# Attention row maxima taken with queries on partitions, the softmax shift carried in two halves, six places for transposed tokens

## The chip, the cores and the metric

The kernel runs on one core of a Trainium2 chip. The metric is device time in microseconds (us) of one execution. The kernel before the change took 273.44 us in the median of 3 runs (272.13 to 273.6).

## The reference

For each of 16 batches of 256 tokens of width 128 the reference does one post-norm transformer layer in float32:

```python
qkv = x @ attn_w.T + attn_b                     # 16 heads of 8; 256 tokens per batch
scores = einsum('bhki,bhqi->bhkq', k, q) / sqrt(8)
scores = where(key <= query, scores, -10000.0)
probs = softmax(scores, axis=key)
x = layernorm(x + (einsum('bhkq,bhkl->bhql', probs, v) heads joined) @ out_w.T + out_b)
# feed-forward: int8 quantised rows of x times int8 quantised columns of rhs
x = layernorm(x + (round(x / sx) @ round(rhs / sr)) * sx * sr)
```

`sx` is the largest absolute value of a token's row over 127, `sr` that of a column of `rhs`.

## The kernel before, in words

Each engine runs its own program, in order, and they meet only at semaphores. All programs walk the same list of phases, b = -4 to 18, and inside a phase the compute engines walk ten units u = 0 to 9. A unit is one PSUM bank of 128 x 512 scores: two halves of 64 partitions (heads 4*half + p%4) and 512 columns. The causal upper triangle of 256 x 256 scores is cut into 64-wide key blocks; FULL, ENDS and THIRD name which key blocks of which head pairs a unit holds. Units 0 to 4 are head pairs 0 to 3 (row tile 0 of the PE array), units 5 to 9 are pairs 4 to 7 (row tile 64).

Scores are computed twice. The first time, for the **maxima**, the bank goes to VectorE (DVE), which takes maxima (`maxima`, L643). The second time, for the **exponentials**, two more rows of the contraction (`DEPTH = ROWS + 2`) subtract a **shift** per group of 32 queries, written as bfloat16 plus remainder, and ScalarE (ACT) exponentiates the bank (L470). `max_unit` sets the lead of the maxima: beside the exponentials of (b, u) PE makes the scores for the maxima of unit u+5, so units 5 to 9 of batch b+1 and then units 0 to 4 of batch b+2. The two kinds use opposite row tiles and run side by side (`scores`).

Before the change both kinds keep keys on partitions, and the maxima go over 32 queries with a transposing reduce. `join_maxima` (after u = 4) reduces over the three kinds of unit, PE turns the result (`turn_maxima`, at u = 5), and `make_shift` (DVE, u = 5) reduces again and makes the two bfloat16 parts. Two DMAs write them into the query rows (`load_shift`, L340), and PE waits for them before the exponentials of the next batch's unit 0 (`bank_for_exp`).

**PSUM rings.** ACT has 4 banks and DVE 3, handed out in the fixed order of `ring_places`: the ten units, and after certain units an extra place (`ACT_EXTRAS`, `DVE_EXTRAS`). PE may fill a place only when the place three back (DVE) or four back (ACT) was emptied. DVE's order has four extras per phase: the output projection after u = 1, the feed-forward after 3, the shift after 5, the turned PV result after 6.

**Who does what in a phase b.** PE, after the scores of the unit named: u = 1 output projection of batch b-2, PV products of b-1, turn of the quantised tokens of b-3; u = 3 query and key projection of b+4 (L933, reads `xt_in`), PV, feed-forward of b-3; u = 5 `turn_maxima(b+1)` and value projection of b+1 (L943, also reads `xt_in`); u = 6 turn of the PV result, PV; u = 8 turn of the heads, PV. DVE has at the matching units the first sum and its statistics (1, 2), the scaling of the feed-forward (3), join (4), shift (5), division by the denominators and the token scale (6), statistics and the second bfloat16 part of q and k (7, 8). GpSimd (POOL) splits q and k into bfloat16 parts and makes the norm factors.

**SP's queue** issues every DMA of the loop, in this order, each waiting for its data in turn:

```python
write_image(b + 3, 1); load_x(b); load_shift(b + 1); read_image(b + 3)
load_xt(b + 5); write_image(b + 4, 0); store(b - 3)
```

`write_image` and `read_image` send the parts of q and k through DRAM into the layout that the scores need. `load_xt(b + 5)` refills one of 4 places of `xt_in` (transposed tokens) and waits until ACT has read the value projection of batch b+1; the query and key projection of b+5 comes in phase b+1 at u = 3. The first four token blocks are loaded ahead of the loop.

Of the kernel before, what the change touches and what calls it, by code (L numbers as in the profile page):

```python
# [59 lines left out]
QK_RING, XT_RING, RING = 4, 4, 3  # L60
# [25 lines left out]

PV_GROUPS = [(0, 1), (2, 3, 4), (5, 6), (7, 8, 9)]
# [7 lines left out]
ACT_EXTRAS = {1: [("zq", -3)], 3: [("q", 4), ("k", 4)], 5: [("v", 1)], 8: [("heads", -1)]}  # L95
DVE_EXTRAS = {1: [("out", -2)], 3: [("ffn", -3)], 5: [("shift", 1)], 6: [("pv", -1)]}
# [38 lines left out]
def build_program(nc, x, xt, wqkv_t, bqkv, wo_t, bo, rhs_t, out):  # L135
    ctx = ExitStack()
    with ctx:
# [26 lines left out]
        causal = sb("causal", [128, KB], BF16)  # L164
        minus_half = sb("minus_half", [128, TILES])
# [62 lines left out]
        shift_loaded = sem("shift_loaded")  # L228
# [44 lines left out]
        POOL_MASK = 9  # L273
# [5 lines left out]
        def _(sp):  # L279
# [6 lines left out]
            for b in range(2, XT_RING):  # L286
                sp.dma_start(xt_in[b][:, :], xt[b]).then_inc(xt_loaded[b], 16)

            def load_xt(b):
                if not real(b) or b < XT_RING:  # L290
# [42 lines left out]
            def load_shift(b):  # L333
                if not real(b):
                    return
                wait_place(sp, dve_emptied, DVE_AT, ("shift", b))
# [26 lines left out]
        def _(pool):  # L363
# [10 lines left out]
            step(pool.memset(causal[:, :], MASKED))  # L374
            step(pool.memset(ones[:, :], 1.0))
# [4 lines left out]
            for half in range(2):  # L380
                m = causal[64 * half:64 * half + 64, :]
                step(pool.affine_select(out=m, in_=m, compare_op=ALU.is_gt, fill=0.0,
                                        base=0, pattern=[[-1, KB]], channel_multiplier=1))
# [79 lines left out]
        def _(act):  # L463
# [112 lines left out]
            def phase(b):  # L576
                for u in range(NU):
                    exponentials(b, u)
                    if u == 1:
                        pv_from_psum(b - 1)  # L580
                        zq_from_psum(b - 3)
                    if u == 3 and b > -4:
                        qk_from_psum(b + 4, 0)
                        qk_from_psum(b + 4, 1)
                    if u == 5:
                        v_from_psum(b + 1)
                        norm1(b - 2)
                    if u == 8:
                        heads_from_psum(b - 1)
                    if u == 9:  # L590
                        round_z(b - 2)
# [5 lines left out]
        def _(dve):  # L597
# [6 lines left out]
            dve.memset(part_max[:, :, :, :], MASKED).then_inc(rows_set, 1)  # L604
# [27 lines left out]
            def maxima(b, u):  # L632
# [5 lines left out]
                first, last = ((0, 8), (2, 10), (4, 8))[kind]  # L638
                out32 = part_max[:, kind, p0:p0 + (4 if kind == THIRD else 2), first:last]
                if u == 0:  # L640
                    wait(dve, max_joined, b - 1)
# [4 lines left out]
            def join_maxima(b):  # L646
                if not real(b):
                    return
                wait_place(dve, dve_emptied, DVE_AT, ("max", b, NU - 1))
                wait_place(dve, dve_filled, DVE_AT, ("shift", b - 1))  # L650
                by_pair = key_max[:, :].rearrange("k (p c) -> k p c", c=8)
                dve.tensor_reduce(by_pair, part_max[:, :, :, 0:8].rearrange("k n p c -> k p c n"),  # L652
                                  op=ALU.max, axis=AX.X).then_inc(max_joined[1], 1)
                wait(dve, max_joined, b, 1)
                dve.tensor_tensor(by_pair[:, :, 6:8], by_pair[:, :, 6:8], part_max[:, 1, :, 8:10],  # L655
                                  ALU.max).then_inc(max_joined[1], 1)
# [6 lines left out]
            def make_shift(b, step):  # L663
# [3 lines left out]
                at = DVE_AT["shift", b]  # L667
                turned = dve_bank[at % DVE_BANKS]
                if step == 0:
                    dve.wait_ge(dve_filled, at + 1)  # L670
                    dve.tensor_reduce(turned[:, 64:96], turned[:, 0:64].rearrange("c (w q) -> c q w", w=2),
                                      op=ALU.max, axis=AX.X, negate=True).then_inc(shift_made[1], 1)
                elif step == 1:
                    wait(dve, shift_made, b, 1)
                    if b > 0:
                        dve.wait_ge(shift_loaded, 32 * b)
                    dve.tensor_copy(shift[:, 0, :], turned[:, 64:96]).then_inc(shift_made[1], 1)
                else:
                    wait(dve, shift_made, b, 2)
                    dve.tensor_tensor(shift[:, 1, :], turned[:, 64:96], shift[:, 0, :],  # L680
                                      ALU.subtract).then_inc(dve_emptied, 1)
# [85 lines left out]
            def phase(b):  # L767
                if b == -3:
                    second_part(1)
                for u in range(NU):  # L770
                    maxima(*max_unit(b, u))
                    if u == 1:
# [4 lines left out]
                    if u == 3:  # L777
                        scale_ffn(b - 3)
                    if u == 4:
                        join_maxima(b + 1)  # L780
                    if u == 5:
                        make_shift(b + 1, 0)
                        make_shift(b + 1, 1)
                        make_shift(b + 1, 2)
# [7 lines left out]
                    if u == 8:  # L792
                        second_stats(b - 3, 1)
# [31 lines left out]
        def _(pe):  # L825
# [14 lines left out]
            def piece_scores(b, u, i, half, bank, depth):  # L840
# [3 lines left out]
                rows, slot = slice(row, row + depth), b % QK_RING  # L844
                pe.matmul(bank[64 * half:64 * half + 64, at:at + TOK - blk * KB],  # L845
                          k_stat[slot][rows, head, blk * KB:(blk + 1) * KB], q_move[slot][rows, head, blk * KB:TOK],
                          start=(at == 0), stop=False, skip_group_check=True)

            def own_blocks(u, half, bank):


                kind, p0 = UNITS[u]
                row, each = TILE_ROWS * (p0 // 4), 1 if kind == FULL else 2
                rows, keys = slice(row, row + KB), slice(64 * half, 64 * half + 64)
                columns = bank[keys, :].rearrange("k (p n q) -> k p n q", p=2, q=KB)[:, :, 0:(1, 4, 4)[kind]:(1, 3, 2)[kind], :]
                return pe.matmul(columns, identb[rows, rows],  # L856
                                 causal[rows, :].unsqueeze(1).unsqueeze(1).to_broadcast([KB, 2, each, KB]),
# [9 lines left out]
            def bank_for_exp(b, u):  # L867
                if u == 0:
                    pe.wait_ge(shift_loaded, 32 * (b + 1))
                return act_ring(("exp", b, u))  # L870

            def scores(b, u):
# [6 lines left out]
                for i in range(len(pieces(u))):  # L879
                    for half in range(2):  # L880
                        if for_max:
                            piece_scores(of_max, unit, i, half, max_bank, ROWS)
                        if for_exp:
                            piece_scores(b, u, i, half, exp_bank, DEPTH)
                for half in range(2):
                    if for_max:
                        own = own_blocks(unit, half, max_bank)
                        if half == 1:
                            own.then_inc(dve_filled, 1)
                    if for_exp:  # L890
                        own = own_blocks(u, half, exp_bank)
# [23 lines left out]
            def turn_maxima(b):  # L915
                if not real(b):
                    return
                wait(pe, max_joined, b)
                bank = dve_ring(("shift", b))
                for s in range(2):  # L920
                    for half in range(2):
                        rows = slice(64 * s + 32 * half, 64 * s + 32 * half + 32)
                        last = pe.matmul(bank[rows, 0:64], key_max[:, 32 * s:32 * s + 32], ident[:, 64 * half:64 * half + 64],  # L923
                                         start=True, stop=True)
                last.then_inc(dve_filled, 1)
# [89 lines left out]
            def phase(b):  # L1015
# [3 lines left out]
                for u in range(NU):  # L1019
# [5 lines left out]
                    if u == 3:  # L1025
                        if b >= -1:
# [47 lines left out]
```

## Time and profile before

| | |
|---|---|
| median of 3 runs | 273.44 us |
| profiled execution, its own time | 273.3 us |
| its span (first to last instruction) | 271.6 us |
| PE busy | 203.1 us, 75% |
| DVE busy | 186.8 us, 69% |
| ACT busy | 161.1 us, 59% |
| POOL busy | 135.2 us, 50% |
| mean granted TensorE clock | 0.952 |

Busy shares are means over a start (to about 42 us), a steady part, and a drain (from about 234 us), and tell little alone. To read a stage, cut the trace at an event that comes once per phase. Here it is the start of DVE's L652, the join after u = 4: it comes at 27.6 us in phase -1 and at 234.3 us in phase 14.

### The profile page before, as it was taken

The page shows a single profiled execution, that of the slowest core. Times are in us where ns is not written, and L with a number is a line of the kernel's source. Part 1 is how long each engine was busy: PE and PEld are TensorE (multiplying, and loading weights), DVE is VectorE, ACT ScalarE, POOL GpSimd, SP SyncE. Part 2 cuts the span into 40 slices and gives each one's busy share as a digit, 9 for nine tenths or more (in the row PEclk, how much of TensorE's full clock was granted, in tenths as well). Part 3 has the DMA queues.
Part 4 walks back from the last instruction along what each step waited for, and adds up shares of the span by engine and source line. Part 5 has one row for each costly group of instructions (what it writes and reads, how often), then busy time and mean ns, then how long its engine had stood idle before and what let it go on. Part 6 is the DMA issues. An engine that isn't in the chain of part 4 may idle for free.

```text
span 271.6 us, 10973 instructions
## 1 busy us (share of the span) xinstructions
PE 203.1 (75%) x4398; PEld 133.9 (49%) x4399; DVE 186.8 (69%) x545; ACT 161.1 (59%) x349; POOL 135.2 (50%) x268
## 2 busy tenths in 40 slices
PE   7269758689886868686878787777778879799610
PEld 4156635456564545454646455545455556565300
DVE  3727834746786869696969696868789899644521
ACT  3811133644685858585767665666767668678420
POOL 7352303231617473737474746474746262445764
PEclk9999999957999999999999999999999999899955
DMA  4499391909283848647675849391929550110001
GB/s 135 160 188 226 68 216 28 230 25 183 94 148 132 139 158 124 175 105 192 104 193 102 196 80 220 66 231 35 242 52 212 108 93 6 42 36 10 19 21 39
DMA packets 50754, 32.82 MB, mean 121 GB/s; under 512 B 7184, under 2 KB 50704, under 8 KB 50704
## 3 DMA queue, kind: packets, MB, share of 16 engines
q1 hardware_dynamic: 50560, 31.93, 52.1%
q8 instruction: 35, 0.57, 0.9%
q10 hardware_dynamic: 144, 0.20, 0.3%
q14 instruction: 15, 0.12, 0.2%
HBM read 17.17 MB, written 14.68 MB: 117 GB/s over the span
## 4 chain that ended last, share of the span: by engine, by line
PE 29%; DMA 25%; DVE 20%; ACT 8%; SPq 7%; issue 7%; POOL 3%; POOLq 0%; ACTq 0%; DVEq 0%
DMA xt_in<-xt_dram 22%; DVE part_max L643 9%; PE act_bank L933 7%; PE pv_bank L910 7%; PE dve_bank L845 4%; ACT z L518 3%; PE act_bank L943 3%; SPq L330 2%; DVE key_max L652 2%; DVE ffn L749 2%; SPq L331 2%; ACT probs L470 2%; DMA k_stat<-imagek 2%; SPq L340 2%; DVE key_max L655 2%
## 5 line engine op out<-in xcount | busy, mean ns | idle before, releaser
L643 DVE TRANSPOSE_TENSOR_REDUCE part_max<-dve_bank 128x16 f32<-128x512 f32 x160 | 108.7, 702 | 31.3 <-PE dve_bank L856 29.4
L470 ACT ACTIVATE probs<-act_bank 128x512 f32<-128x512 f32 x160 | 88.3, 595 | 31.1 <-PE act_bank L856 30.3
L845 PE MATMUL dve_bank<-q_move,k_stat 48*64 48x256 bf16 (+3 forms) x1024 | 67.1, 251 | 2.0 <-DMA k_stat<-imagek 1.8
L845 PE MATMUL act_bank<-q_move,k_stat 50*64 50x256 bf16 (+3 forms) x1024 | 63.6, 242 | 0.0
L845 PEld LDWEIGHTS dve_bank<-q_move,k_stat 48*64 48x64 bf16 x1024 | 42.5, 115 | 22.5 <-issue 10.2
L910 PE MATMUL pv_bank<-probs,v_stat 128*32 128x256 f32 (+3 forms) x1024 | 50.6, 318 | 0.3 <-ACT probs L470 0.2
L856 PE MATMUL dve_bank<-causal,identb 64*64 64x256 bf16 (+1 forms) x320 | 44.4, 270 | 0.6 <-issue 0.6
L856 PE MATMUL act_bank<-causal,identb 64*64 64x256 bf16 (+1 forms) x320 | 42.3, 260 | 0.0
L422 POOL TENSOR_SCALAR rstd<-moments 128x2 f32<-128x2 f32 x32 | 7.4, 230 | 69.3 <-DVE moments L765 53.8
L845 PEld LDWEIGHTS act_bank<-q_move,k_stat 50*64 50x64 bf16 x1024 | 39.9, 111 | 1.6 <-issue 0.6
L933 PE MATMUL act_bank<-xt_in,wqkv 128*128 128x256 f32 x64 | 22.6, 490 | 14.7 <-DMA xt_in<-xt_dram 14.3
L404 POOL TENSOR_TENSOR qk_parts<-qk_rest,qk_parts 128x512 bf16<-128x512 f32 x15 | 17.4, 1157 | 27.8 <-DVE qk_parts L661 27.8
L910 PEld LDWEIGHTS pv_bank<-probs,v_stat 128*32 128x32 f32 x1024 | 22.8, 113 | 15.9 <-issue 5.1
L482 ACT ACTIVATE qk_f<-act_bank,bias 128x256 f32<-128x256 f32 x30 | 13.1, 474 | 25.7 <-PE act_bank L933 25.6
L494 ACT ACTIVATE v_stat<-act_bank 64x256 f32<-64x256 f32 x32 | 12.1, 378 | 25.7 <-PE act_bank L943 25.5
L749 DVE SCALAR_TENSOR_TENSOR ffn<-dve_bank,zscale,rhs_scale 128x128 f32<-128x128 f32 x32 | 9.6, 342 | 20.9 <-PE dve_bank L994 20.9
L424 POOL TENSOR_TENSOR rstd<-rstd,minus_half 128x2 f32<-128x2 f32 x32 | 22.4, 700 | 2.7
L933 PEld LDWEIGHTS act_bank<-xt_in,wqkv 128*128 128x128 f32 x64 | 13.5, 231 | 20.0 <-DMA xt_in<-xt_dram 15.8
L856 PEld LDWEIGHTS dve_bank<-causal,identb 64*64 64x64 bf16 x320 | 20.2, 118 | 0.2
L923 PE MATMUL dve_bank<-ident,key_max 128*32 128x64 f32 x128 | 5.5, 246 | 19.8 <-DVE key_max L655 19.8
L856 PEld LDWEIGHTS act_bank<-causal,identb 64*64 64x64 bf16 x320 | 18.8, 112 | 0.9 <-issue 0.8
L399 POOL TENSOR_TENSOR qk_rest<-qk_f,qk_parts 128x512 f32<-128x512 f32 x15 | 17.4, 1157 | 1.2
(87 smaller groups left out, 312.4 us busy)
## 6 DMA issues: line engine op xcount, KB each, us to landing
imageq<-qk_parts SPq DMA_DIRECT2D x32, 192.0 KB, 3.6
imagek<-qk_parts SPq DMA_DIRECT2D x32, 192.0 KB, 4.0
q_move<-imageq SPq DMA_DIRECT2D x32, 192.0 KB, 3.9
k_stat<-imagek SPq DMA_DIRECT2D x32, 192.0 KB, 4.5
xt_in<-xt_dram SPq DMA_DIRECT2D x16, 128.0 KB, 4.8
x_in<-x_dram SPq DMA_DIRECT2D x16, 128.0 KB, 3.5
out_dram<-o SPq DMA_DIRECT2D x16, 128.0 KB, 3.1
q_move<-shift SPq DMA_DIRECT2D x32, 8.0 KB
```

The lines of the kernel that those rows point to most:

```text
L399: pool.tensor_tensor(qk_rest[:, :, :], qk_f[:, :, :], first, ALU.subtract).then_inc(qk_split[1], 1)
L404: pool.tensor_tensor(third, qk_rest[:, :, :], second, ALU.subtract).then_inc(qk_split[1], 1)
L424: pool.tensor_tensor(t[:, 0, :], t[:, 0, :], minus_half[:, :], ALU.pow).then_inc(made[1], 1)
L470: act.activation(probs[u][:, :], act_bank[at % ACT_BANKS][:, :], ACT.Exp, scale=SCALE).then_inc(act_emptied, 1)
L482: act.activation(qk_f[:, w, :], src, ACT.Identity, bias=bias[:, w:w + 1]).then_inc(act_emptied, 1)
L494: last = act.activation(v_stat[b % RING][half, :, :, 16 * s:16 * s + HD], src, ACT.Copy)
L643: dve.tensor_reduce(out32, dve_bank[at % DVE_BANKS][:, :].rearrange("k (c q) -> k c q", q=32), op=ALU.max, axis=AX.X, apply_transpose=True ...
L749: last = dve.scalar_tensor_tensor(out=ffn[:, t, :], in0=dve_bank[at % DVE_BANKS][:, t * DIM:(t + 1) * DIM], scalar=zscale[:, 1, t:t + 1], ...
L845: pe.matmul(bank[64 * half:64 * half + 64, at:at + TOK - blk * KB], k_stat[slot][rows, head, blk * KB:(blk + 1) * KB], q_move[slot][rows, ...
L856: return pe.matmul(columns, identb[rows, rows], causal[rows, :].unsqueeze(1).unsqueeze(1).to_broadcast([KB, 2, each, KB]), start=False, st ...
L910: last = pe.matmul(pv_bank[col:col + 32, p // 4, blk * KB:TOK], v_stat[b % RING][:, blk, p, :], probs[u][:, at:at + TOK - blk * KB], start ...
L933: pe.matmul(bank[:, 0:TOK], wqkv[:, w, :], xt_in[b % XT_RING][:, :], start=True, stop=True).then_inc(act_filled, 1)
```

## The change

The scores for the maxima are transposed: queries become the stationary operand and keys the moving one, so queries stand on partitions and an ordinary reduce along the free dimension ends each maximum (per block of 64 queries now). Which key blocks make a unit is mirrored, with the same number of columns per unit, and the mask has a transposed twin. The maxima are joined, turned and made into a shift for each half of the heads (row tile) separately, each half with its own place in DVE's ring (five extras per phase) and its own semaphore. `xt_in` has six places. Projections and DMAs move: value projection from u = 5 to u = 8, `load_xt` one phase earlier, and in phase -1 the query and key projection from u = 3 to u = 8.

```diff
-QK_RING, XT_RING, RING = 4, 4, 3
+QK_RING, XT_RING, RING = 4, 6, 3
+XT_FIRST = 4
+def max_pieces(u):
+    kind, p0 = UNITS[u]
+    if kind == FULL:
+        return [(p0 + j, 3, TOK * j) for j in range(2)]
+    if kind == ENDS:
+        return [(p0 + j, blk, TOK * j + at) for j in range(2) for blk, at in ((2, KB), (0, 0))]
+    return [(p0 + j, 1, 2 * KB * j) for j in range(4)]
-ACT_EXTRAS = {1: [("zq", -3)], 3: [("q", 4), ("k", 4)], 5: [("v", 1)], 8: [("heads", -1)]}
-DVE_EXTRAS = {1: [("out", -2)], 3: [("ffn", -3)], 5: [("shift", 1)], 6: [("pv", -1)]}
+ACT_EXTRAS = {1: [("zq", -3)], 3: [("q", 4), ("k", 4)], 8: [("heads", -1), ("v", 1)]}
+DVE_EXTRAS = {1: [("out", -2)], 3: [("shift0", 1), ("ffn", -3)], 6: [("pv", -1)], 8: [("shift1", 1)]}
-        part_max = sb("part_max", [128, 3, PAIRS, 10])
-        key_max = sb("key_max", [128, 64])
-        shift = sb("shift", [128, 2, 32], BF16)
+        ends_max = sb("ends_max", [128, PAIRS, 6])
+        query_max = sb("query_max", [128, PAIRS, 4])
+        shift = [sb(f"shift{s}", [16, 2, 128], BF16) for s in range(2)]
...
# SP
+            def load_shift(b, s):
...
                 for part in range(2):
-                    row = ROWS + part
-                    sp.dma_start(q_move[b % QK_RING][row:row + TILE_ROWS + 1:TILE_ROWS, :, :].rearrange("s f (c q) -> s (f c) q", q=32),
-                                 shift[:, part, :]).then_inc(shift_loaded, 16)
+                    row = s * TILE_ROWS + ROWS + part
+                    for half in range(2):
+                        heads_of_half = q_move[b % QK_RING][row:row + 1, 4 * half:4 * half + 4, :]
+                        sp.dma_start(heads_of_half.rearrange("r j t -> r (j t)"), shift[s][:, part, 64 * half:64 * half + 64]).then_inc(shift_loaded[s], 16)
             def phase(b):
                 write_image(b + 3, 1)
+                load_shift(b + 1, 0)
                 load_x(b)
-                load_shift(b + 1)
+                if b < 0:
+                    load_shift(b + 1, 1)
                 read_image(b + 3)
-                load_xt(b + 5)
+                load_xt(b + 6)
                 write_image(b + 4, 0)
+                if b >= 0:
+                    load_shift(b + 1, 1)
                 store(b - 3)
# DVE: maxima, join, shift
-                dve.tensor_reduce(out32, dve_bank[at % DVE_BANKS][:, :].rearrange("k (c q) -> k c q", q=32),
-                                  op=ALU.max, axis=AX.X, apply_transpose=True).then_inc(dve_emptied, 1)
+                dve.tensor_reduce(top, keys, op=ALU.max, axis=AX.X).then_inc(dve_emptied, 1)
+            def join_maxima(b, s):
...
+                wait_place(dve, dve_emptied, DVE_AT, ("max", b, 5 * s + 4))
+                dve.tensor_reduce(query_max[:, pairs, 0:4:2], ends_max[:, pairs, :].rearrange("q p (n k) -> q p n k", n=2),
+                                  op=ALU.max, axis=AX.X).then_inc(max_joined[1], 1)
+            def make_shift(b, s):
...
+                turned = dve_bank[at % DVE_BANKS][0:16, 0:128]
+                dve.wait_ge(dve_filled, at + 1)
+                if b > 0:
+                    dve.wait_ge(shift_loaded[s], 64 * b)
+                dve.tensor_scalar(shift[s][:, 0, :], turned, -1.0, None, ALU.mult).then_inc(shift_made[1], 1)
+                wait(dve, shift_made, b, s + 1)
+                dve.scalar_tensor_tensor(out=shift[s][:, 1, :], in0=turned, scalar=-1.0, in1=shift[s][:, 0, :],
+                                         op0=ALU.mult, op1=ALU.subtract).then_inc(dve_emptied, 1)
# DVE, phase: joins after u = 0 (half 0) and u = 5 (half 1) in place of u = 4;
#             shifts after u = 3 (half 0) and u = 8 (half 1) in place of u = 5
# ACT, phase: v_from_psum(b + 1) after u = 8 in place of u = 5
# PE
+            def max_scores(b, u, i, half, bank):
+                p, blk, at = max_pieces(u)[i]
+                row, head = TILE_ROWS * (p // 4), 4 * half + p % 4
+                rows, slot, keys = slice(row, row + ROWS), b % QK_RING, (blk + 1) * KB
+                pe.matmul(bank[64 * half:64 * half + 64, at:at + keys],
+                          q_move[slot][rows, head, blk * KB:keys], k_stat[slot][rows, head, 0:keys],
+                          start=(i == 0), stop=False, skip_group_check=True)
             def bank_for_exp(b, u):
-                if u == 0:
-                    pe.wait_ge(shift_loaded, 32 * (b + 1))
+                if u == 0 or u == 5:
+                    pe.wait_ge(shift_loaded[u // 5], 64 * (b + 1))
+            def turn_maxima(b, s):
...
+                bank = dve_ring((f"shift{s}", b))
+                pe.matmul(bank[0:16, 0:128], query_max[:, 4 * s:4 * s + 4, :].rearrange("q p n -> q (p n)"), ident[:, :],
+                          start=True, stop=True).then_inc(dve_filled, 1)
                     if u == 3:
-                        if b >= -1:
+                        turn_maxima(b + 1, 0)
+                        if b >= 0:
                             project_qk(b + 4, 0)
                             project_qk(b + 4, 1)
-                    if u == 5:
-                        turn_maxima(b + 1)
-                        project_v(b + 1)
                     if u == 8:
+                        turn_maxima(b + 1, 1)
+                        if b == -1:
+                            project_qk(b + 4, 0)
+                            project_qk(b + 4, 1)
                         turn_heads(b - 1)
+                        project_v(b + 1)
```

## Rows read from the trace of the kernel before

**Rows 1.** The page's chain that ended last, share of the span by line.

```profile
DMA xt_in<-xt_dram 22%; DVE part_max L643 9%; PE act_bank L933 7%; PE pv_bank L910 7%; PE dve_bank L845 4%; ACT z L518 3%; PE act_bank L943 3%; SPq L330 2%; DVE key_max L652 2%; DVE ffn L749 2%; SPq L331 2%; ACT probs L470 2%; DMA k_stat<-imagek 2%; SPq L340 2%; DVE key_max L655 2%
```

**Rows 2.** The chain from 138 to 168 us: start us, us, what.

```profile
152.57 1.13 PE act_bank L933 x4
...
157.88 0.52 SPq L340
...
161.32 5.68 DMA xt_in<-xt_dram
```

**Rows 3.** Windows cut at L652's starts: busy us (count) by engine, clock, DMA.

```profile
core 0: us, PE busy (x) PEld busy (x) DVE busy (x) ACT busy (x) POOL busy (x), PEclk, DMA share, GB/s
...
27.60:42.60 15.00, 11.09 (x168) 7.77 (x168) 8.10 (x16) 4.75 (x10) 4.49 (x6) 1.00 0.55 125
42.60:57.60 15.00, 11.71 (x260) 7.41 (x260) 7.97 (x16) 7.64 (x16) 4.17 (x6) 0.89 0.56 126
57.60:72.00 14.40, 12.84 (x270) 8.67 (x270) 9.92 (x25) 7.92 (x17) 3.57 (x8) 0.76 0.59 131
...
85.60:99.80 14.20, 10.96 (x274) 7.26 (x274) 11.19 (x34) 9.63 (x22) 8.41 (x17) 1.00 0.66 143
...
184.40:198.50 14.10, 10.96 (x274) 7.26 (x274) 11.17 (x34) 9.60 (x22) 8.39 (x17) 1.00 0.58 144
...
222.50:234.30 11.80, 10.08 (x268) 6.69 (x267) 10.60 (x33) 9.16 (x20) 4.85 (x13) 1.00 0.13 33
```

**Rows 4.** Waits, whole span: engine line waited for, total us, times, longest.

```profile
PE dve_bank L923 <- DVE key_max L655: 19.8, 16, 1.5
...
PE act_bank L933 <- DMA xt_in<-xt_dram: 14.3, 12, 2.7
```

**Rows 5.** DVE's timeline in one steady phase: start, us, [idle before it].

```profile
141.05 0.71 DVE L643 TRANSPOSE_TENSOR_REDUCE part_max<-dve_bank 128x16 f32<-128x512 f32 x1
...
145.32 0.42 DVE L732 TENSOR_REDUCE zscale<-z 128x2 f32<-128x256 f32 x1 [0.41 <-ACT z L518]
...
148.22 1.91 DVE L643 TRANSPOSE_TENSOR_REDUCE part_max<-dve_bank 128x16 f32<-128x512 f32 x3
...
151.43 0.72 DVE L643 TRANSPOSE_TENSOR_REDUCE part_max<-dve_bank 128x16 f32<-128x512 f32 x1 [0.47 <-PE dve_bank L856]
...
154.53 0.61 DVE L749 SCALAR_TENSOR_TENSOR ffn<-dve_bank,zscale,rhs_scale 128x128 f32<-128x128 f32 x2 [1.65 <-PE dve_bank L994]
155.06 0.70 DVE L643 TRANSPOSE_TENSOR_REDUCE part_max<-dve_bank 128x16 f32<-128x512 f32 x1
```

**Rows 6.** DVE by line and form: shapes, count, busy us, mean ns.

```profile
L643 DVE TRANSPOSE_TENSOR_REDUCE part_max<-dve_bank 128x16 f32<-128x512 f32 x160 | 108.7, 702 | 31.3 <-PE dve_bank L856 29.4
L749 DVE SCALAR_TENSOR_TENSOR ffn<-dve_bank,zscale,rhs_scale 128x128 f32<-128x128 f32 x32 | 9.6, 342 | 20.9 <-PE dve_bank L994 20.9
...
L732 DVE TENSOR_REDUCE zscale<-z 128x2 f32<-128x256 f32 x16 | 6.7, 418 | 8.5 <-ACT z L518 8.5
...
L652 DVE TENSOR_REDUCE key_max<-part_max 128x64 f32<-128x192 f32 x16 | 6.1, 381 | 0.5
...
L655 DVE TENSOR_TENSOR key_max<-key_max,part_max 128x16 f32<-128x16 f32 x16 | 4.4, 273 | 0.6
...
L671 DVE TENSOR_REDUCE dve_bank<-dve_bank 128x32 f32<-128x64 f32 x16 | 3.3, 203 | 0.4 <-PE dve_bank L923 0.4
```

**Rows 7.** PE's timeline in the same phase.

```profile
149.08 0.68 PE L975 MATMUL dve_bank<-wo,heads_d 128*128 128x128 f32 x4 [0.75 <-DVE part_max L643]
...
152.57 0.48 PE L933 MATMUL act_bank<-xt_in,wqkv 128*128 128x256 f32 x1 [0.84 <-DMA xt_in<-xt_dram]
```

**Rows 8.** Shift and token transfers: issue durations, landing, the first shift's landing.

```profile
L340 SPq DMA_DIRECT2D q_move<-shift x32: 512/517/660, 29.8 to 236.6; - x32
...
DMA to landing us min/median/max: 4.2/5.1/5.7
...
29.83 1.22 SPq L340 DMA_DIRECT2D q_move<-shift  x2
...
32.54 0.42 PE L845 MATMUL act_bank<-q_move,k_stat 50*64 50x256 bf16 x1
```

More of the change, by code:

```diff
@@ L227, in build_program @@
         qk_loaded = [sem(f"qk_loaded{i}") for i in range(QK_RING)]
-        shift_loaded = sem("shift_loaded")
+        shift_loaded = [sem(f"shift_loaded{s}") for s in range(2)]
         stored = sem("stored")
@@ L285, in _ @@
             sp.dma_start(rhst[:, :], rhs_t).then_inc(rhs_in, 16)
-            for b in range(2, XT_RING):
+            for b in range(2, XT_FIRST):
                 sp.dma_start(xt_in[b][:, :], xt[b]).then_inc(xt_loaded[b], 16)
             def load_xt(b):
-                if not real(b) or b < XT_RING:
+                if not real(b) or b < XT_FIRST:
                     return
@@ L380, in _ @@
             for half in range(2):
[L381 to L383 removed]
+                for m, sign in ((causal, 1), (causal_t, -1)):
+                    m = m[64 * half:64 * half + 64, :]
+                    step(pool.affine_select(out=m, in_=m, compare_op=ALU.is_gt, fill=0.0,
+                                            base=0, pattern=[[-sign, KB]], channel_multiplier=sign))
             assert done[0] == POOL_MASK, done[0]
@@ L646, in join_maxima @@
-            def join_maxima(b):
+                if kind == FULL:
+                    top = query_max[:, p0:p0 + 2, 3]
+                elif kind == ENDS:
+                    top = ends_max[:, p0:p0 + 2, 2:6]
+                else:
+                    top = query_max[:, p0:p0 + 4, 1]
+                if u == 0 or u == 5:
+                    wait_place(dve, dve_filled, DVE_AT, (f"shift{u // 5}", b - 1))
+                dve.wait_ge(dve_filled, at + 1)
+                keys = dve_bank[at % DVE_BANKS][:, :]
@@ L771, in phase @@
                     maxima(*max_unit(b, u))
+                    if u == 0:
+                        join_maxima(b + 1, 0)
                     if u == 1:
@@ L838, in dve_ring, with exp_scores, own_blocks @@
                 return dve_bank[at % DVE_BANKS]
-            def piece_scores(b, u, i, half, bank, depth):
+            def exp_scores(b, u, i, half, bank):
                 p, blk, at = pieces(u)[i]
                 row, head = TILE_ROWS * (p // 4), 4 * half + p % 4
-                rows, slot = slice(row, row + depth), b % QK_RING
+                rows, slot = slice(row, row + DEPTH), b % QK_RING
                 pe.matmul(bank[64 * half:64 * half + 64, at:at + TOK - blk * KB],
                           k_stat[slot][rows, head, blk * KB:(blk + 1) * KB], q_move[slot][rows, head, blk * KB:TOK],
[L847 to L855, printed above, removed]
+                          start=(i == 0), stop=False, skip_group_check=True)
[5 more added lines that the diff above has]
+                          q_move[slot][rows, head, blk * KB:keys], k_stat[slot][rows, head, 0:keys],
+                          start=(i == 0), stop=False, skip_group_check=True)
+            def own_blocks(u, half, bank, own, mask):
+                row = TILE_ROWS * (UNITS[u][1] // 4)
+                rows, out = slice(row, row + KB), slice(64 * half, 64 * half + 64)
+                columns = bank[out, :].rearrange("k (p n q) -> k p n q", p=2, q=KB)[:, :, own, :]
                 return pe.matmul(columns, identb[rows, rows],
-                                 causal[rows, :].unsqueeze(1).unsqueeze(1).to_broadcast([KB, 2, each, KB]),
+                                 mask[rows, :].unsqueeze(1).unsqueeze(1).to_broadcast([KB, 2, 1 if UNITS[u][0] == FULL else 2, KB]),
                                  start=False, stop=True, skip_group_check=True)
@@ L890, in scores @@
                     if for_exp:
-                        own = own_blocks(u, half, exp_bank)
+                        own = own_blocks(u, half, exp_bank, EXP_OWN[UNITS[u][0]], causal)
                         if half == 1:
@@ L913, in pv @@
                 last.then_inc(pv_done[1], 1)
-            def turn_maxima(b):
+            def turn_maxima(b, s):
                 if not real(b):
                     return
[L918 to L925, printed above, removed]
+                wait(pe, max_joined, b, s + 1)
+                bank = dve_ring((f"shift{s}", b))
+                pe.matmul(bank[0:16, 0:128], query_max[:, 4 * s:4 * s + 4, :].rearrange("q p n -> q (p n)"), ident[:, :],
+                          start=True, stop=True).then_inc(dve_filled, 1)
             def project_qk(b, w):
```

60 lines of the change are left out of this document (20 added, 40 removed).

## The prediction, as put on record before the changed kernel was run

> **What bounds the kernel now.** I read the chain of waits first. Its largest line is the load of the transposed tokens, 22% of the span [rows 1], though no engine is 80% busy. Over one steady phase the chain is a closed loop [rows 2]: query and key projection at 152.57, some DVE work, the issue of the shift's DMAs at 157.88, the four reads of the image queued behind them on SP, the token load issued at 161.32, which takes 5.68 us, and the next projection. SP's order makes the loop: `load_xt(b+5)` stands behind the shift of the same phase, and the projection that needs it comes at u = 3 of the next.
>
> Then the windows. From 85.60 to 198.50 lie eight phases, 14.11 us each, with DVE busy for 11.2 and PE for 10.96; in 222.50:234.30, which has neither loads nor projections of q and k, a phase takes 11.80 with DVE at 10.60 [rows 3]. PE waits 14.3 us in all for tokens, over 12 projections [rows 4]. That number is not what the loop costs: part of its slack sits at other waits. The three early phases are 15.0, 15.0 and 14.4 us with DVE busy for only 8.10, 7.97 and 9.92 [rows 3]: there the loop costs most.
>
> Last, DVE's timeline, for what binds when the loop is gone. I cut a phase at three starts of L643: u=4 at 141.05, u=9 at 148.22, u=2 at 151.43, u=4 again at 155.06 [rows 5], so C (u=4 to 9) = 7.17, A (9 to 2) = 3.21, B (2 to 4) = 3.63.
>
> **The change, part by part.**
>
> *Six places, load a phase earlier.* The load now has over a phase to land, against 5.7 us at most [rows 8]. PE's 0.84 us before the projection goes [rows 7], out of stretch B. Without it B is 2.8.
>
> *Projection, turn and shift in B.* After the scores of u=3 PE now has the first turn as well: one small product in place of four; I take 0.15 us more. B becomes 2.95. DVE sat idle for 1.65 us of it [rows 5], 0.8 with the wait gone, and the new shift of half 0 falls there: two operations over 128 columns of PSUM. A line through 64 columns at 203 ns and 256 at 418 gives 0.28 for 128; L749, of the second one's kind, has 342 [rows 6]. Together 0.6 to 0.65. DVE fills B with max, moments, max (2 x 0.61 + 0.15), shift 0.65 and feed-forward 0.55: 2.6. B stays PE's, 2.95.
>
> *A.* PE starts the output projection when a bank comes free (it waited 0.75 for DVE [rows 7]), then PV and a turn; DVE idles 0.47 at the end [rows 5]. The join of half 0 (24 columns per pair group, about 0.2 by L671) eats into that 0.47. A stays 3.2.
>
> *C* is DVE's: it is idle there for 0.41 only [rows 5]. Out go the join (381 + 273 ns [rows 6]), the shift's three operations (at most 0.2 each, L671 being one), some 0.2 of gaps for their dependences, and the 0.41, an ACT operation that stood behind the value projection, itself behind PE's wait of 19.8/16 = 1.2 us for the join [rows 4]. That is 0.65 + 0.6 + 0.2 + 0.41 = 1.9. In come one join (0.2) and one shift (0.65). C becomes 7.17 - 1.9 + 0.85 = 6.1. The value projection at u=8 adds 0.6 us to PE there, which DVE covers with a maximum, a shift, moments and the second part of q and k; if it didn't, C would be 0.3 longer.
>
> *The reduce itself.* The transposing one takes 702 ns, 0.61 from start to start. The line above gives 0.69 for 512 columns: no gain, no loss. Bounds: twice the 256-column one, 0.84, and that one alone, 0.42. I take 0.70. Same columns and as many weight loads on PE: nothing.
>
> A steady phase is then 3.2 + 2.95 + 6.1 = 12.25 us, saving 1.86, and over eight phases 14.9.
>
> *Start.* Moving the projection of batch 3 behind u=8 in phase -1 brings its join's place forward by about 2 us; second parts of batch 3 then hold DVE for some 4 us later, half hidden. By the windows I put phase -1 to 0 at 14.7, 0 to 1 at 11.5 (PE is busy for 11.7 of the 15, much of it at doubled matmul times), 1 to 2 at 11.9 (PE had a clock of 0.76 there [rows 3] after waits that go), 2 to 3 at 12.0 from 13.6. Sum with the 2 us: 2 + 0.3 + 3.5 + 2.5 + 1.6 = 9.9 saved; bounds 5 and 14.
>
> *Tail.* Three phases without loads: C's gain less what A and B keep, 0.2 each, 0.6. The drain keeps its chain.
>
> Total 14.9 + 9.9 + 0.6 = 25.4. The profiled execution took 273.3 us (span 271.6), 0.1 under the median: 273.3 - 25.4 = 247.9.
>
> *What SP pays.* Eight shift transfers in place of two, 0.517 us of issue each [rows 8]: 3.1 more per phase. SP then issues 19 transfers, some 9.5 us of 12.25. Half 0's four go out before the image reads, whose own data arrive later anyway; half 1's go out after `write_image(b+4, 0)`. The last one starts some 2.6 us after u=9 and is needed 6.3 us after it (A plus B plus a little), so 3.7 us remain for landing.
> What can be said of landing: the first shift's pair was issued in 29.83 to 31.05 and PE used it at 32.54 [rows 8], so a small transfer lands in 2.0 us or less on a quiet queue. Upper bound: the longest token load, 5.7. I take 2 to 3, nearest to the same kind of transfer.
>
> The Trainium skill speaks against this part: DMA: Bandwidth & Descriptors, section Rules for kernel authors, wants many small transfers joined into one, since below 64 KB one pays mostly overhead, which its section on the anatomy of one DMA puts at about 2.0 us each. Were these costs paid one after another, eight would be 16 us a phase, and the kernel slower. The row speaks for overlap: two shift transfers were issued and usable within 2.7 us.
>
> **Rivals.**
> 1. *Only the loop goes.* The halves gain nothing: C keeps its 7.1 because the two shifts cost what was removed, or PE's work at u=8 shows. For: DVE gets four shift operations for three. Against: PE's 1.2 us wait for the join and the 0.41 vanish. Phase 3.2 + 2.8 + 7.15 = 13.15, 7.7 over eight phases, start 8: 257.5.
> 2. *Half 1's shift lands late*, at about 4.5 us behind 384 KB of image writes on the same queue; PE stalls for 0.8 at u=5 of every phase, 12 times: 257. For: the write is just ahead of it in the queue, and large transfers take over 4 us. Against: the loads before it are issued 2 us sooner.
> 3. *Better than forecast*: the plain reduce's pitch is 0.55 and the start gains its 14: 242.
> 4. *Slower than before.* Shift transfers to a single partition land in over 5.6 us. From 3.7 us on each microsecond is a PE stall before the exponentials of u=5; at 3.7 + 1.86 = 5.6 a steady phase is as long as before. At 7 us a phase is 15.5: 273.3 + 8 x 1.4 - 5 = 280. The longest landing seen, 5.7, only just reaches the point, and those are 128 KB.
> 5. *The loop stays*: SP, with 19 issues, is late enough for tokens or images to bind again: 270 to 273. Against: the token load has a whole phase of slack.
>
> **How the numbers follow.** Forecast 0.60 (its own range 243 to 252), rival 1 0.14, rival 2 0.10, rival 3 0.08, rival 4 0.05, rival 5 0.03. The range is 241 to 258: it takes in the forecast and rivals 1 to 3. About 0.5% of the time, 1.4 us, is what a measurement can tell from none. Faster is everything but rival 4 and half of rival 5: 0.93; same 0.02; slower 0.05.
>
> **What the profile would show.** Chain: the token load's share near zero past the start, DVE and PE in its place. Windows: starts of the maxima of one unit 12.0 to 12.5 us apart in the middle, DVE busy for 11.2 to 11.5. Waits: PE for tokens at most 2 us, PE for the join near none. DVE: the reduce at 0.68 to 0.72, shift operations 0.28 and 0.34, idle 0.2 to 0.3 before u=2, little before the feed-forward. PE stalls before exponentials of u=5 would mean rival 2 or 4. A middle phase of 13 us without any such stall would mean that C was sized wrong. A reduce of over 0.8, or a start that ends after 80 us (u=4 of phase 3, before at 85.6), would break the sum.

## The result and the profile after

The changed kernel took 253.92 us in the median of 4 runs (250.72 to 258.24), against 273.52 for the kernel before beside it: ratio 0.919, 95% interval 0.912 to 0.926. The forecast was 247.9, range 241 to 258. The profiled execution took 250.7 us (span 249.0). Runs of one kernel scatter by some us, so experiments are compared by their ratio to the kernel before on the same chip. Medians are of all runs, ratios of the fast ones alone, and four profiled executions are slow ones, so that their phases and waits may be longer for it (places only, both kernels with the load at b+5, the second shift on ACT).

The page's chain that ended last, answering to [rows 1]. The token load is gone, and the transfer of the shift stands first.

```profile
DMA q_move<-shift 11%; PE pv_bank L940 9%; PE dve_bank L873 7%; DVE query_max L672 7%; SPq L356 6%; PE act_bank L959 3%; DVE ends_max L672 3%; PE act_bank L864 2%; PE dve_bank L883 2%; PE dve_bank L950 2%; PE act_bank L969 2%; DMA k_stat<-imagek 2%; PE dve_bank L1001 2%; PE dve_bank L983 2%; DVE stats L779 2%
```

Windows as in [rows 3], now cut at the starts of the second half's join (DVE L680 after u = 5).

```profile
26.73:41.55 14.82, 13.63 (x192) 8.98 (x190) 7.60 (x19) 6.16 (x13) 5.78 (x7) 1.00 0.51 119
41.55:52.35 10.80, 9.15 (x256) 5.94 (x244) 7.88 (x19) 7.57 (x16) 4.17 (x5) 1.00 0.75 175
52.35:64.58 12.23, 10.52 (x268) 7.08 (x266) 9.48 (x26) 7.83 (x18) 5.16 (x9) 1.00 0.62 156
76.77:88.62 11.85, 11.15 (x272) 7.39 (x270) 10.73 (x35) 9.61 (x23) 8.16 (x16) 1.00 0.71 170
101.06:114.22 13.16, 11.20 (x272) 7.40 (x270) 10.74 (x36) 9.62 (x23) 9.39 (x18) 1.00 0.65 153
153.07:166.57 13.50, 11.24 (x273) 7.41 (x271) 10.72 (x35) 9.46 (x22) 10.13 (x19) 1.00 0.62 150
166.57:179.56 12.99, 12.44 (x272) 8.09 (x270) 10.83 (x36) 9.71 (x23) 6.68 (x15) 0.87 0.60 145
```

In the middle phases at full clock DVE and PE do the same work (10.7 and 11.2 to 11.4 us; at the clock of 0.87 PE's is 12.44), yet phases last from 11.85 to 13.50; the eight from 76.77 to 179.56 have a mean of 12.85, where 12.25 was forecast. DVE's timeline of one that waits, answering to [rows 5]:

```profile
105.36 1.27 DVE L672 TENSOR_REDUCE query_max<-dve_bank 128x4 f32<-128x512 f32 x2
...
108.53 0.69 DVE L672 TENSOR_REDUCE ends_max<-dve_bank 128x8 f32<-128x512 f32 x1 [0.36 <-PE dve_bank L883]
...
111.03 0.61 DVE L768 SCALAR_TENSOR_TENSOR ffn<-dve_bank,zscale,rhs_scale 128x128 f32<-128x128 f32 x2 [0.58 <-PE dve_bank L1020]
111.56 0.68 DVE L672 TENSOR_REDUCE query_max<-dve_bank 128x4 f32<-128x512 f32 x1
113.61 0.69 DVE L672 TENSOR_REDUCE query_max<-dve_bank 128x2 f32<-128x512 f32 x1 [1.37 <-PE dve_bank L883]
```

A, from u=9 at 105.36 to u=2, is 3.17, B is 3.03 with 0.58 idle in place of 1.65. Then, before u=5, DVE waits 1.37 us for PE, and PE's timeline names its cause:

```profile
113.03 0.27 PE L873 MATMUL dve_bank<-k_stat,q_move 48*64 48x256 bf16 x1 [1.58 <-DMA q_move<-shift]
```

The queue that issues these transfers, SP's timeline over the same place (start, duration):

```profile
112.73 2.40 SPq L356 DMA_DIRECT2D q_move<-shift  x4
115.17 0.58 SPq L313 DMA_DIRECT2D x_in<-x_dram  x1
115.85 0.42 SPq L344 DMA_DIRECT2D q_move<-imageq  x1
116.31 1.51 SPq L345 DMA_DIRECT2D k_stat<-imagek  x1
117.87 0.47 SPq L344 DMA_DIRECT2D q_move<-imageq  x1
118.38 0.47 SPq L345 DMA_DIRECT2D k_stat<-imagek  x1
118.90 0.47 SPq L307 DMA_DIRECT2D xt_in<-xt_dram  x1
119.47 0.38 SPq L327 DMA_DIRECT2D imageq<-qk_parts  x1
119.89 0.43 SPq L327 DMA_DIRECT2D imagek<-qk_parts  x1
120.42 2.42 SPq L356 DMA_DIRECT2D q_move<-shift  x4
122.89 1.28 SPq L362 DMA_DIRECT2D out_dram<-o  x1
124.21 0.46 SPq L327 DMA_DIRECT2D imageq<-qk_parts  x1
124.72 0.45 SPq L327 DMA_DIRECT2D imagek<-qk_parts  x1
```

No gap between its rows is longer than 0.1 us. Summed over such rows (one of several transfers holds the short gaps inside it), SP issued for 54.1 of 112.9 us in the middle of the kernel before (104 transfers, 0.52 each) and for 93.7 of 102.8 us in the changed one (150, 0.62 each). And the waits and landings, whole span. All eight waits stand before the exponentials of u = 5, so for the second half's shift; the landings that can be told in this trace are the first half's alone:

```profile
PE dve_bank L873 <- DMA q_move<-shift: 10.9, 8, 2.2
```

```profile
L356 SPq DMA_DIRECT2D q_move<-shift x128: 502/589/1903, 24.4 to 219.7; - x128
...
DMA to landing us min/median/max: 1.6/2.1/3.4
```

The second profile of the same kernel (changed, again) tells both halves' landings:

```profile
DMA to landing us min/median/max: 1.6/2.4/4.1
```

Taken apart there, the first half's land in 1.8 us (median) and the second half's, those that PE waits for, in 3.1.

DVE's costs, answering to [rows 6]:

```profile
L672 DVE TENSOR_REDUCE query_max<-dve_bank 128x2 f32<-128x512 f32 x64 | 43.5, 682 | 14.8 <-PE dve_bank L883 14.7
L672 DVE TENSOR_REDUCE ends_max<-dve_bank 128x8 f32<-128x512 f32 x64 | 42.9, 680 | 6.8 <-PE dve_bank L883 6.8
...
L699 DVE SCALAR_TENSOR_TENSOR shift<-dve_bank,shift 16x128 bf16<-16x128 f32 x32 | 8.9, 279 | 1.1
L697 DVE TENSOR_SCALAR shift<-dve_bank 16x128 bf16<-16x128 f32 x32 | 8.6, 269 | 0.0
...
L680 DVE TENSOR_REDUCE query_max<-ends_max 128x8 f32<-128x24 f32 x32 | 5.3, 165 | 0.0
```

### The profile page after: what moved, and what is told of

Read it like the earlier page. It is cut to its first block, busy times and chain, and to the rows that moved or that the text cites. A ratio compares the mean times of both kernels' runs of the same rounds, so it can differ in the third digit from the quotient of the medians.

```text
span 249.0 us, 11019 instructions
## 1 busy us (share of the span) xinstructions
PE 203.3 (82%) x4334; PEld 134.1 (54%) x4335; DVE 181.1 (73%) x561; ACT 160.6 (64%) x349; POOL 135.8 (55%) x271
## 4 chain that ended last, share of the span: by engine, by line
PE 36%; DVE 19%; DMA 15%; issue 9%; SPq 7%; POOL 4%; ACT 3%; POOLq 0%; DVEq 0%; ACTq 0%
DMA q_move<-shift 11%; PE pv_bank L940 9%; PE dve_bank L873 7%; DVE query_max L672 7%; SPq L356 6%; PE act_bank L959 3%; DVE ends_max L672 3%; PE act_bank L864 2%; PE dve_bank L883 2%; PE dve_bank L950 2%; PE act_bank L969 2%; DMA k_stat<-imagek 2%; PE dve_bank L1001 2%; PE dve_bank L983 2%; DVE stats L779 2%
## 5 line engine op out<-in xcount | busy, mean ns | idle before, releaser
L491 ACT ACTIVATE probs<-act_bank 128x512 f32<-128x512 f32 x160 | 89.3, 594 | 41.3 <-PE act_bank L883 40.6
L672 DVE TENSOR_REDUCE query_max<-dve_bank 128x2 f32<-128x512 f32 (+1 forms) x96 | 63.8, 682 | 22.0 <-PE dve_bank L883 22.0
L873 PE MATMUL dve_bank<-k_stat,q_move 48*64 48x256 bf16 (+3 forms) x1024 | 64.1, 249 | 16.8 <-DMA q_move<-shift 10.9
L873 PEld LDWEIGHTS dve_bank<-k_stat,q_move 48*64 48x64 bf16 x1024 | 42.8, 115 | 36.4 <-issue 19.8
L864 PE MATMUL act_bank<-q_move,k_stat 50*64 50x256 bf16 (+3 forms) x1024 | 60.7, 240 | 0.7 <-issue 0.7
L672 DVE TENSOR_REDUCE ends_max<-dve_bank 128x8 f32<-128x512 f32 x64 | 42.9, 680 | 6.8 <-PE dve_bank L883 6.8
L883 PE MATMUL dve_bank<-causal_t,identb 64*64 64x256 bf16 (+1 forms) x320 | 44.6, 268 | 0.0
L883 PEld LDWEIGHTS dve_bank<-causal_t,identb 64*64 64x64 bf16 x320 | 20.5, 116 | 1.0 <-issue 0.8
L418 POOL CAST qk_parts<-qk_f 128x512 bf16<-128x512 f32 x15 | 9.1, 610 | 18.9 <-ACT qk_f L503 17.4
```

The source lines that it names most:

```text
L491: act.activation(probs[u][:, :], act_bank[at % ACT_BANKS][:, :], ACT.Exp, scale=SCALE).then_inc(act_emptied, 1)
L672: dve.tensor_reduce(top, keys, op=ALU.max, axis=AX.X).then_inc(dve_emptied, 1)
L873: pe.matmul(bank[64 * half:64 * half + 64, at:at + keys], q_move[slot][rows, head, blk * KB:keys], k_stat[slot][rows, head, 0:keys], start ...
L883: return pe.matmul(columns, identb[rows, rows], mask[rows, :].unsqueeze(1).unsqueeze(1).to_broadcast([KB, 2, 1 if UNITS[u][0] == FULL else ...
```

## The experiments

Theory: the token loop is gone, and SP's nearly full queue has taken its place, through the second half's shift. Rivals: small transfers to one partition take long to land wherever they stand; or the gain came from one part alone.

Mean middle phase is over eight phases, from phase 3 on, of the profiled run, one execution per kernel. The last column is in us over the span; "-" is a view without such a wait.

| kernel | ratio (95%) | median us | middle phase | PE waits for shift |
|---|---|---|---|---|
| changed, again | 0.920 (0.908 to 0.931) | 253.4 | 12.66 | 10.3 |
| places only | 0.944 (0.931 to 0.957) | 260.9 | 13.76 | - |
| load at b+5 | 0.914 (0.899 to 0.930) | 254.5 | 13.26 | 4.5 |
| shift before image write | 0.911 (0.900 to 0.922) | 251.3 | 12.65 | 12.2 |
| second shift on ACT | 0.921 (0.907 to 0.936) | 255.1 | 12.94 | 2.0 |
| two transfers on ACT | 0.903 (0.897 to 0.909) | 246.2 | 12.18 | 8.2 |
| two idle issues added | 0.971 (0.965 to 0.978) | 265.1 | 14.23 | 24.2 |
| two on ACT, shift first | 0.888 (0.881 to 0.895) | 241.8 | 12.24 | 3.9 |
| the same, load at b+5 | 0.908 (0.900 to 0.917) | 248.3 | 12.70 | - |
| changed, start undone | 0.939 (0.931 to 0.947) | 256.2 | 13.10 | 13.7 |
| two on ACT, first, start undone | 0.884 (0.878 to 0.890) | 241.2 | 11.82 | 0.5 |
| and the token load on ACT | 0.875 (0.868 to 0.883) | 240.2 | 11.80 | 1.3 |

**The changed kernel again**, no edit. 

> The changed kernel itself, as the measure for the others on the same chip: 250 to 256, ratio to the kernel before 0.91 to 0.93.

It repeats the result. Each experiment below edits this kernel, but for places only.

**Places only**, made on the kernel before:

```diff
-QK_RING, XT_RING, RING = 4, 4, 3
+QK_RING, XT_RING, RING = 4, 6, 3
-                load_xt(b + 5)
+                load_xt(b + 6)
```

> The kernel before, with six token places and load_xt(b + 6) in place of b + 5, and nothing else of the change. If the token loop was worth what the cut of the phase said (A 3.2, B 2.8, C 7.15), a middle phase is 13.1 to 13.2 us and the time about 257 (the start saves 8 of it). If the halves bring nothing of their own, this kernel equals the changed one (251 in its undisturbed runs). If the loop only hid another wait, 268 or more.

The loop goes: PE waits for no token, and four of the five middle phases at full clock take 13.34 or 13.35 us (the fifth 13.06), 0.2 above the 13.15 of the prediction. The three with a lower clock are dearer:

```profile
100.38:113.72 13.34, 10.89 (x274) 7.26 (x274) 11.41 (x33) 9.48 (x22) 8.34 (x17) 1.00 0.63 151
113.72:128.28 14.56, 12.21 (x274) 8.16 (x274) 11.47 (x34) 9.52 (x22) 8.34 (x17) 0.88 0.63 139
```

So the places and the earlier load are worth 0.056 of the time, the rest of the change 0.025 more. They are not the whole gain, as rival 1 would have had it.

**Load at b+5** in the changed kernel, places kept. 

> The changed kernel with load_xt(b + 5) again, six places kept, so that no place is waited for. The load is then issued at the end of the image reads, about 4 us before its projection, and takes 4.7 to land. If the earlier phase of the load matters: PE waits for tokens by 0.5 to 1 us in most phases, 254 to 262. If the first half's shift, now ahead of the reads, was what opened the loop, no change: 250 to 252.

PE waited 11.2 us for tokens in 7 waits and only 4.5 for the shift, and the ratio was that of the changed kernel within its interval. One wait stood in for the other, as if something else set the pace; this run alone does not show what.

**Shift before the image write**, in the changed kernel:

```diff
-                write_image(b + 4, 0)
                 if b >= 0:
                     load_shift(b + 1, 1)
+                write_image(b + 4, 0)
```

> The changed kernel with the second half's shift issued before write_image(b + 4, 0) instead of behind it. Theory: PE's waits before the exponentials of u = 5 (10.9 us in 8 waits) come from its place on SP's queue, which is nearly full. Then it goes out about 1 us sooner and no longer behind 384 KB: the waits shrink to under 3 us, middle phases go to 11.9 us, the time to 244 to 247. Rival: the landing of a transfer to one partition is long by itself: waits of 6 us or more stay and the time is 249 to 251. Second rival: the image write that is now 2.4 us later makes PE wait for k_stat or q_move: no gain, and a new wait on the image.

The theory's number failed: PE still waited 12.2 us for the shift, and the middle phase is 12.65 against 12.66. The second half's shift did go out sooner, 1.41 us after DVE had made it in the mean of eight phases against 2.00. But the first half's went out later, 2.15 against 1.33, and the second half's landed later, at a median of 3.5 us against 3.1. Moving one block within a full queue makes another late; which of these kept the waits up is not shown. The ratios (0.911 against 0.920, on different chips) overlap.

**Second shift on ACT's queue**: `load_shift(b + 1, 1)` issued by ACT after u = 9. 

> The changed kernel with the second half's four transfers issued by ACT after u = 9. Theory of the full SP queue: SP drops to 15 issues and PE's waits for the shift go. ACT pays 4 issues of 0.5 to 0.6 us, 9.6 + 2.3 = 11.9 us busy or blocked per phase, about the phase itself: 246 to 251, with PE waiting for ACT's banks in place of the shift. If ACT's issues cost it much less than 0.5 us: 244.

PE's wait for the transfers nearly goes, and SP waits for DVE's shift again (22.9 us), though the second half's land no sooner (median 3.1). But the phase settled at 12.31 to 12.33 in four of the eight, and PE now waits 7.4 us for ACT to empty a bank, against 1.0 in the changed kernel again; ACT's issues took 0.61 us each (median). No gain: issue time on a busier engine.

**Two transfers on ACT**, in the changed kernel:

```diff
# SP: load_x(b) and store(b - 3) removed; ACT, phase(b):
+                    if u == 4:
+                        store(b - 4)
+                    if u == 7:
+                        load_x(b)
+            store(NBATCH - 1)    # after the last phase
```

> The changed kernel with the load of x (after u = 7) and the store of the result (after u = 4) issued by ACT, so that SP issues 17 transfers per phase and not 19. Theory: SP's queue, busy for 103.8 of 114.4 us in the middle of the changed kernel, paces it. Then 1.1 to 1.2 us per phase come off SP, middle phases go from 12.8 to 11.9 us, ACT goes from 9.6 to 10.8 us and stays under the phase: 8 to 11 us off, ratio 0.88 to 0.89. Rival (landing of the shift transfers by itself): PE's waits for them stay at 10 us, ratio as the changed kernel. Rival (ACT in order): a wait of ACT for the store costs as much as SP gains.

Ratio 0.903, 4.6 us better than the changed kernel beside it, by intervals that just touch; about half of what the theory said. PE's waits for the shift only fell to 8.2. What is left is the order: SP takes up the second half's shift behind an image write whose data DVE makes last, and in five of eight middle phases it went out 1.47 us after it was made, as it does at the earliest in the changed kernel.

**Two idle issues** on SP, of the shift's form, into a place nobody reads:

```diff
                 store(b - 3)
+                if real(b):
+                    for i in range(2):
+                        sp.wait_ge(idle_sent[i], 16 * b) if b else sp.wait_ge(idle_set, 1)
+                        sp.dma_start(idle_to[i][:, :], idle_from[:, :]).then_inc(idle_sent[i], 16)
```

> The changed kernel with two more transfers per phase on SP's queue, of the form of the shift's (16 x 64 to one partition) and into a place that nobody reads. Theory of the full queue: 2 x 0.6 us on SP for 12 to 14 phases make the time 12 to 16 us longer, ratio 0.96 to 0.98. Rival (SP has slack, landing decides): under 2 us longer, ratio as the changed kernel.

The clearest test: 0.052 of the time, 14 us, for transfers with no reader; a middle phase is 1.57 us longer, where the two issues take 0.68 each. SP issued for 107.4 of 113.8 us, and PE waited more for a shift whose own transfers were unchanged: the second half's landed in 3.0 us (median, 3.1 without the idle ones), but went out 3.4 us after DVE had made them, against 2.0.

```profile
PE dve_bank L884 <- DMA q_move<-shift: 24.2, 12, 4.0
```

**Two on ACT and the shift before the image write.** 

> The kernel with two transfers on ACT's queue and besides the second half's shift issued before write_image(b + 4, 0). With the queue no longer full the order should matter at last: if the last waits for the shift come from the writes ahead of it, another 1 to 3 us off, ratio 0.87 to 0.88; if the queue's length was all, the same as with two on ACT alone.

0.888 against 0.903: the order that did nothing in the full queue is worth 0.015 in one with room. The second half's shift now goes out 0.55 us after it is made, in place of 1.83.

**The same with the load at b+5.** 

> The kernel with x and the store on ACT's queue and the second shift ahead of the image write, but with load_xt(b + 5) again (six places kept). With the changed kernel's full queue the later load made no difference that could be told. If that was because the queue paced both, it must show here: PE waits for tokens, 4 to 10 us more than with b + 6 (ratio 0.90 to 0.92 against 0.888). If the earlier load is worth nothing once the first half's shift goes out at u = 3: the same ratio, 0.88 to 0.89.

0.908 against 0.888, and PE waits 8.6 us for tokens. So the earlier load counts, once the queue doesn't hide it.

**Start undone**: in the changed kernel the projection of batch 3 is at u = 3 of phase -1 again. 

> The changed kernel with the query and key projection of batch 3 at u = 3 of phase -1, as before. In the kernel with only the places added, the start reached phase 0's u = 4 at 38.6 us, in the changed one at about 40.9, where DVE waits 4.2 us for POOL's split of batch 3. Theory: the moved projection costs the start 2 to 3 us, ratio 0.91. Rival: it pays, as it lets the first exponentials start sooner, and undoing it costs 1 us or more.

The theory was wrong and the rival right, by more than it said: 0.939 against 0.920 (0.919 in the first four runs, whose interval is clear of it). PE waits 4.2 us for k_stat, against 1.8, the second half's join of phase 3 comes at 79.47 us in place of 76.77, and the middle phases, 13.10, are longer as well, though nothing in them was edited. Why a queue-bound loop keeps a worse rhythm after another start was not settled.

**Both**: two on ACT, shift first, start undone. 

> Two transfers on ACT's queue, the second shift ahead of the image write, and the projection of batch 3 at u = 3 of phase -1. If the start's 2 to 3 us and the queue's add up: ratio 0.875 to 0.88, about 239; if the time gained in the start is lost at the first shift waits, 0.888.

0.884, the same as with the moved start: no sum of gains, but no loss either. So the moved start is worth something only where the queue is full, as far as these runs show. The middle runs at what DVE and PE need of each other: 11.69 or 11.70 in six of eight phases. DVE's timeline there:

```profile
151.31 1.27 DVE L675 TENSOR_REDUCE query_max<-dve_bank 128x4 f32<-128x512 f32 x2
...
154.48 0.69 DVE L675 TENSOR_REDUCE ends_max<-dve_bank 128x8 f32<-128x512 f32 x1 [0.37 <-PE dve_bank L886]
...
157.51 1.28 DVE L675 TENSOR_REDUCE query_max<-dve_bank 128x4 f32<-128x512 f32 x2
158.71 0.17 DVE L683 TENSOR_REDUCE query_max<-ends_max 128x8 f32<-128x24 f32 x1
```

**The token load on ACT too**, after u = 6. 

> As the kernel with both, and the token load on ACT's queue too (after u = 6), so SP issues 16 per phase. If the rest of the shift waits (3.9 us with 17) still comes from the queue's length, middle phases go to 11.7 throughout, 2 to 3 us off: ratio 0.865 to 0.875. ACT is then at 11.4 of 11.7 us with its issues; if that binds, the time is the same or 2 us longer.

The best kernel, 240.2 us, though its interval reaches into that of the one before. Against the landing rival it has the decisive rows. The landings that can be told here are the second half's, and they take 3.2 us (median), as they did in the changed kernel again (3.1), whose PE waited 10.3 us. Here PE waits for them once.

```profile
PE dve_bank L877 <- DMA q_move<-shift: 1.3, 1, 1.3
```

```profile
L343 SPq DMA_DIRECT2D q_move<-shift x128: 502/589/2070, 24.6 to 209.3; - x128
...
DMA to landing us min/median/max: 1.6/3.2/4.2
```

## Why the prediction was right, and where it was not

*The token loop* [rows 2]. Right, and shown by the places alone: 13.34 us against 13.15 forecast.

*A and B.* Right: 3.17 and 3.03 against 3.2 and 2.95; the first half's shift fell into DVE's idle time before the feed-forward, as forecast.

*C*, forecast at 6.1. Without waits it is 11.70 - 3.17 - 3.03 = 5.50. The shift's pair takes 0.51 from the first start to the next operation (150.27 to 150.78 in the kernel with both) where 0.65 was priced, the join 0.08 where 0.2 was. The five reduces of C take 3.00 from start to start, before 3.28, 0.28 for which nothing was counted. The unhindered phase is thus 11.7, better than forecast, and DVE is busy for 10.7 of it where 11.2 to 11.5 was forecast.

*The reduce.* 682 ns against 0.70: next to no gain, as said. (The line through 203 and 418 ns gives 0.71 for 512 columns, not 0.69.)

*The start.* The u=5 reduce of phase 3 began at 76.16, before at 86.35: 10.2 saved, 9.9 forecast. Its intervals of 14.8, 10.8, 12.2 and 12.2 answer to 14.7, 11.5, 11.9 and 12.0. In its parts this was partly luck: I counted 2 us gained by the moved projection, and what it gains is only visible when it is undone: 2.7 us by the join of phase 3 in the changed kernel, none in the one with two transfers on ACT (75.67 with it, 75.82 without).

*What SP pays* is the step that failed. It set 19 issues at some 9.5 us of 12.25, half a microsecond each, and put the start of half 1's last transfer 2.6 us after u = 9, which left 3.7 for landing. (The kernel before alone gives 9.9: 54.1 us in eight phases and 3.1 more in each.) Transfers took 0.62 on average and the 13 gaps between the rows of a turn some 0.7 together, so SP needed 11.8 + 0.7 = 12.5 us per phase, more than the 11.7 that the compute engines need. With 17 issues at 0.65 it is the same as those 11.7.

In the phase shown, DVE had the second half's shift ready at 104.9, its first transfer went out at 107.63 and the last at 109.44, 4.1 after u = 9. It had landed by 112.79, 3.34 later, inside the 3.7 allowed though above the 2 to 3 taken, and PE stood from 111.45 to 113.03. This is rival 2's stall at rival 2's place, but what tips it is the wait before the issue, 2.7 us, not the landing. Some 1.5 of the 2.7 is the place behind the image write, which the 2.6 of the prediction about held; the other 1.2 is the queue. Its price in the middle was 12.85 - 11.7 = 1.15 us per phase, 9 us in all. That the number came out near is in part luck: C, forecast 0.6 too long, hid about half of that price.

*The sum.* The span fell by 22.6: 10.2 in the start, 10.2 over the eight middle phases where 14.9 was forecast, 2.2 after them where 0.6 was. The miss of 2.8 in the profiled execution is thus 4.7 from the middle phases, less what the others gave; against the median of the four runs the miss is 6.0.

The Trainium skill, DMA: Bandwidth & Descriptors, section Issuing engines are not separate DMA queues, says that issuing from several engines saves only the time that the sequencer takes to initiate a DMA, usually small beside the DMA itself. The trace agrees: a load of x or a store is issued in 0.58 us and lands in 2.8 or 2.7. Yet where those issues fill the queue, 1.2 us per phase off SP was worth 4.6 us. The 2.0 us that the prediction took from the same page of the Trainium skill, section Anatomy of one DMA, stands there for DMAs issued by GpSimd, and these are issued by SP. The landings here had a least value of 1.6 and medians of 1.8 and 3.1 for the two halves, and they overlapped: the four issued from 112.73 on had all landed by 116.27.

## What to carry to other kernels

Add up the issue time of every DMA on a queue per loop turn, at the durations that new shapes can have and with the gaps, and compare it with the turn that the change aims at: a queue at 48% becomes the bound when a change both adds issues and shortens the turn. The share alone does not tell: in the kernel with both, SP issued for 87.9 of 94.6 us, a share as high as in the changed kernel, and PE waited 0.5 us for the shift. When a wait names a small transfer, look first at when it was issued after its data was ready; and when moving that transfer brings nothing while adding an unrelated issue costs its full time (1.57 us a phase for two), the queue is what binds.

## What was not expected of the hardware

The average issue took longer: 0.52 us before, 0.62 in the changed kernel. Part of it is the mix, since 8 of 19 are now shift transfers, with a median of 0.589 where the old ones had 0.517. The rest is single issues of more than 1 us (up to 1.8), 16 of 149 in the middle of the changed kernel against 5 of 104 before. Nothing run here shows why.

PE's granted clock was 0.87 or 0.88 in single phases in the middle of a kernel. Cut finer, each holds a stretch at 0.50, the lower of the two levels (1.2 GHz in place of 2.4), and each such stretch comes behind waits of PE. Windows of 1 us of the changed kernel (PE's wait for the shift ends at 138.8), as in [rows 3]:

```profile
137.00:138.00 1.00, 0.37 (x20) 0.15 (x12) 1.00 (x3) 0.49 (x1) 0.97 (x2) 1.00 0.73 232
138.00:139.00 1.00, 0.20 (x8) 0.23 (x12) 0.16 (x1) 0.11 (x1) 0.92 (x2) 1.00 0.81 299
140.00:141.00 1.00, 1.00 (x12) 0.42 (x14) 1.00 (x5) 1.00 (x4) 0.72 (x2) 0.50 0.10 20
```

Not every such wait was followed by one: the clock stayed at 1.00 after the wait that ended at 113.03. The kernel with both, where those waits are gone, kept 1.00 through all eight middle phases. In the kernel with only the places a phase with such a stretch was 1.2 us longer. In the changed kernel the two (13.08 and 12.99) were within the spread of the others, as a phase that waits for the queue would be.
